# Group statistics, maxima and bias summed on VectorE by turning 32x32 squares, in a linear-attention block

## What is computed

```python
g = (x - mean_G(x)) / sqrt(var_G(x) + 1e-5)      # over the positions and the 8 channels of a group
q, k, v = split(g @ W_qkv)                        # 256 columns each
k = softmax(k, axis=n)                            # over the 4096 positions
context = einsum('nd,ne->de', k, v)
out = x + einsum('de,nd->ne', context, q) @ W_out + b_out
```

## Time and profile before

| | us |
|---|---|
| median of 3 runs | 1215.44 (1214.12 to 1215.74) |
| the profiled execution | 1214.93 |
| span in its trace, first to last instruction | 1213.2 |
| outside the span | 1.7 |

### The profile page before, as it was taken

The page is one execution under the profiler, slowest core; times in us unless marked ns, Lnnn a source line. Parts: engine busy times, 40 slices in busy tenths (PEclk is TensorE's granted clock), DMA queues, the critical chain, the costliest instruction groups (busy, mean ns, idle before and its releaser), DMA issues.

```text
span 1213.2 us, 21447 instructions
## 1 busy us (share of the span) xinstructions
PE 1190.1 (98%) x8460; PEld 1115.8 (92%) x8460; DVE 842.1 (69%) x1582; ACT 840.1 (69%) x1140; POOL 622.4 (51%) x288
## 2 busy tenths in 40 slices
PE   4999999999999999999999999999999999999998
PEld 4998999999899998999989999899999989999897
DVE  6877667676776767768776677766767676676551
ACT  5767768677685776757677686776857768577664
POOL 8664564635645355563655636356463564536520
PEclk9999999999999999999999999999999999999999
DMA  9448666576765758666486665867657576573524
GB/s 339 146 167 294 218 235 205 195 269 208 274 203 199 264 172 294 226 206 237 162 301 229 221 227 183 286 209 252 204 201 263 193 278 225 201 252 122 191 74 170
DMA packets 107077, 266.71 MB, mean 220 GB/s; under 512 B 10208, under 2 KB 10208, under 8 KB 106976
## 3 DMA queue, kind: packets, MB, share of 16 engines
q1 hardware_dynamic: 106976, 265.33, 63.5%
HBM read 198.18 MB, written 67.11 MB: 219 GB/s over the span
## 4 chain that ended last, share of the span: by engine, by line
PE 93%; DVE 2%; ACT 1%; POOL 1%; DMA 1%; issue 1%; SPq 0%; DVEq 0%; POOLq 0%; ACTq 0%
PE ps_k L399 29%; PE ps_e L564 19%; PE ps_e L573 10%; PE ps_g L492 5%; PE ps_e L480 5%; PE ps_e L492 5%; PE ps_e L482 5%; PE ps_g L480 4%; PE ps_g L482 4%; PE ps_g L511 1%; PE ps_g L528 1%; PE ps_g L542 1%; PE ps_g L534 1%; POOL x_lo L347 1%; DVE mx L892 1%
## 5 line engine op out<-in xcount | busy, mean ns | idle before, releaser
L341 POOL TENSOR_TENSOR xt_lo<-xt_raw,xt_hi 128x1024 fp32r<-128x1024 f32 x128 | 307.4, 2404 | 434.5 <-ACT xt_hi L676 309.1
L347 POOL TENSOR_TENSOR x_lo<-x_raw,x_hi 128x1024 fp32r<-128x1024 f32 x128 | 281.4, 2216 | 65.6 <-ACT x_hi L681 56.2
L892 DVE TENSOR_TENSOR mx<-ps_k,mx 128x256 f32<-128x256 f32 x480 | 203.3, 424 | 95.8 <-ACT e_raw L685 74.3
L733 ACT ACTIVATE o_stage<-ps_e,bias 128x512 f32<-128x512 f32 x253 | 170.9, 689 | 114.1 <-PE ps_e L573 114.1
L399 PE MATMUL ps_k<-wk_hi,xt_hi 128*128 128x256 f32 x1024 | 207.1, 284 | 1.0 <-DVE mx L892 0.7
L399 PE MATMUL ps_k<-wk_lo,xt_hi 128*128 128x256 f32 x1024 | 205.5, 283 | 0.0
L685 ACT ACTIVATE e_raw<-ps_k 128x512 f32<-128x512 f32 x256 | 141.4, 596 | 87.2 <-PE ps_k L399 87.2
L849 DVE BATCH_NORM_STATS2 bn<-xs 128x6 f32<-128x512 f32 x240 | 154.5, 686 | 40.7 <-DMA xs<-in_xt_dram 39.5
L693 ACT ACTIVATE e_hi<-e_raw 128x1024 fp32r<-128x1024 f32 x128 | 135.1, 1055 | 60.9 <-DVE e_raw L917 33.0
L399 PEld LDWEIGHTS ps_k<-wk_hi,xt_hi 128*128 128x128 f32 x1024 | 163.4, 190 | 8.7 <-issue 1.8
L399 PE MATMUL ps_k<-wk_hi,xt_lo 128*128 128x256 f32 x1024 | 158.2, 283 | 0.0
(11 more groups left out here) (129 smaller groups left out, 1992.7 us busy)
## 6 DMA issues: line engine op xcount, KB each, us to landing
xt_raw<-in_xt_dram SPq DMA_DIRECT2D x128, 512.0 KB, 4.3
x_raw<-in_xn_dram SPq DMA_DIRECT2D x128, 512.0 KB, 3.5
out_dram<-o_stage SPq DMA_DIRECT2D x127, 512.0 KB, 4.5
xs<-in_xt_dram SPq DMA_DIRECT2D x240, 256.0 KB, 5.1
w_setup<-in_w_dram SPq DMA_DIRECT2D x2, 256.0 KB, 10.1
out_dram<-o_stage SPq DMA_DIRECT2D x2, 256.0 KB, 2.0
wk<-in_w_dram SPq DMA_DIRECT2D x1, 256.0 KB, 9.9
wq_t<-in_w_dram SPq DMA_DIRECT2D x1, 256.0 KB, 10.9
```

What stands on the lines that cost most here:

```text
L341: nc.gpsimd.tensor_tensor(xt_lo[:, s], xt_raw[:, s], xt_hi[:, s].bitcast(F32), ALU.subtract).then_inc(xt_lo_ready, 1)
L347: nc.gpsimd.tensor_tensor(x_lo[:, s], x_raw[:, s], x_hi[:, s, :, 0:C].bitcast(F32), ALU.subtract).then_inc(x_lo_ready, 1)
L733: nc.scalar.activation(o_stage[:, u % O_SLOTS, h, :], src, ACT.Identity, bias=bias[:, h:h + 1]).then_inc(o_ready, 1)
L892: nc.vector.tensor_tensor(mx[:], tile, mx[:], ALU.max).then_inc(max_done, 1)
```

## The change

The averages over groups, the maxima and the bias no longer pass through TensorE, but for one matmul a block that spreads the maximum. In place of the 128x128 turn, VectorE turns 32x32 squares (`nc.vector.transpose`), so channel 32q+i comes to partition i of each quarter; it reduces along the row, moves the three upper quarters of the partitions down to the first (`move`, a reduction over one element), and reduces again. `block_diag` then writes the maxima (high and low part) on the diagonals of 64 x 256, and `spread_max` becomes one float32r matmul with ones. `group_sum` does the same for the group averages: turn, sum 8 neighbours, repeat each 8 times, turn back. `bias_of` is now a weighted sum over partitions of `ps_g0`, made by the same steps. Scales of the two blocks (`alpha`) are made on 32 partitions and spread by four moves. The last two statistics slices of the next image and `bn_sum` move from the end of the keys stage into the gather; `take_first` moves behind `e_low(b, 6)`. GpSimd waits for `diag_ready` ahead of two of its subtractions, and `rstd_of` moves two places back. ScalarE prepares two constants at the start. The same happens for image 0, whose order is written out apart.

```diff
-            def turn_max(b, blk):
-
-                to = max_psum(b, blk)
-                pe.wait_ge(max_done, b * (TILES * NCH) + TILES * HALF * (blk + 1))
-                for d in range(CB):
-                    last = nc.tensor.transpose(to[:, 0, d * P:(d + 1) * P], mx[:, d * P:(d + 1) * P], ident)
-                last.then_inc(t_ps, 1)
-
             def spread_max(b, blk):
 
-                to = max_psum(b, blk)
-                pe.wait_ge(m_blk_ready, b * 2 + (blk + 1))
-                for d in range(CB):
-                    last = nc.tensor.matmul(to[:, 1, d * P:(d + 1) * P],
-                                            m_blk[:, blk, d:d + 1].broadcast_to([P, P]), ident,
-                                            start=(d == 0), stop=True, skip_group_check=True)
-                last.then_inc(bc_ps, 1)
-
+                pe.wait_ge(diag_ready, b * 2 + (blk + 1))
+                nc.tensor.matmul(max_psum(b, blk)[:, 1, 0:C], one_r[0:2 * Q].broadcast_to([2 * Q, P]), diag,
+                                 start=True, stop=True).then_inc(bc_ps, 1)
...
-            def bias_sum(b, parity):
-                pe.wait_ge(m_full_ready, b + 1)
-                for h in range(CB):
-                    for c in range(CB):
-                        last = nc.tensor.matmul(ps_g0[:, 0, h:h + 1], m_full[:, c, h * P:(h + 1) * P],
-                                                neg_mean[:, parity, c:c + 1], start=(h == 0 and c == 0),
-                                                stop=(c == CB - 1), skip_group_check=True)
-                last.then_inc(bias_ps, 1)
...
                 n, np_ = b + 1, 1 - parity
+                pool.wait_ge(diag_ready, b * 2 + 2)
                 if more:
                     xt_low(n, np_, 0)
-                    if b:
-                        rstd_of(n, np_)
                 for j in range(HALF, NCH):
                     x_low(b, j)
-                    if b == 0 and j == NCH - 2:
+                    if more and j == (NCH - 2 if b == 0 else NCH - 3):
                         rstd_of(n, np_)
                 if more:
                     pool.wait_ge(wk_ready, n + 1)
@@ -388,6 +415,8 @@
                     for j in range(X_SLOTS):
                         x_low(n, j)
                     for j in range(3, NCH):
+                        if j == HALF + 1:
+                            pool.wait_ge(diag_ready, n * 2 + 1)
                         xt_low(n, np_, j)
 
...
+            def move(to, values):
+
+                return nc.vector.tensor_reduce(to, values.unsqueeze(len(values.shape)), AX_X, ALU.max)
...
+            def group_sum(n):
+
+
+                nc.vector.transpose(st_turned[:], st[:]).then_inc(st_turned_ready, 1)
+                dve.wait_ge(st_turned_ready, n)
+                nc.vector.tensor_reduce(st_sum[:], st_turned[:].rearrange("p (g i) -> p g i", i=GC), AX_X,
+                                        ALU.add).then_inc(st_sum_ready, 1)
+                dve.wait_ge(st_sum_ready, n)
+                move(st_held[:].rearrange("p (g i) -> p g i", i=GC),
+                     st_sum[:].unsqueeze(2).broadcast_to([P, Q // GC, GC])).then_inc(st_held_ready, 1)
+                dve.wait_ge(st_held_ready, n)
+                nc.vector.transpose(st_group[:], st_held[:]).then_inc(st_group_ready, 1)
+                dve.wait_ge(st_group_ready, n)
+
+            def stats_of(b, parity):
+                dve.wait_ge(mv_ready, b + 1)
+                group_sum(2 * b + 1)
+                mean_sum = st_group[:, 0:2 * CB].rearrange("p (c s) -> p c s", c=CB)[:, :, 0]
+                nc.vector.scalar_tensor_tensor(out=dev[:], in0=mean_sum, scalar=-1.0 / GC, in1=mv[:, :, 0],
+                                               op0=ALU.mult, op1=ALU.add)
+                nc.vector.tensor_scalar(neg_mean[:, parity, :], mean_sum, -1.0 / GC, None, ALU.mult).then_inc(mean_read, 1)
+                dve.wait_ge(var2_ready, b + 1)
+                group_sum(2 * b + 2)
+                nc.vector.tensor_scalar(var_eps[:], st_group[:, 2 * CB:3 * CB], 1.0 / GC, EPS, ALU.mult,
+                                        ALU.add).then_inc(var_eps_ready, 1)
...
             def block_max(b, blk):
-                src = max_psum(b, blk)
-                dve.wait_ge(t_ps, b * 2 + (blk + 1))
-                nc.vector.tensor_reduce(m_blk[:, blk, :], src[:, 0, 0:C].rearrange("p (d n) -> p d n", d=CB),
-                                        AX_X, ALU.max).then_inc(m_blk_ready, 1)
+
+
+                n = b * 2 + blk + 1
+                dve.wait_ge(max_done, n * (TILES * HALF))
+                nc.vector.transpose(turned[:], mx[:]).then_inc(turned_ready, 1)
+                dve.wait_ge(turned_ready, n)
+                nc.vector.tensor_reduce(quad[:, :, 0], turned[:].rearrange("p (q k) -> p q k", k=Q), AX_X,
+                                        ALU.max).then_inc(quad_ready, 1)
+                dve.wait_ge(quad_ready, n)
+                for r in range(1, QUADS):
+                    last = move(quad[0:Q, :, r], quad[r * Q:(r + 1) * Q, :, 0])
+                last.then_inc(quad_moved, 1)
+                dve.wait_ge(quad_moved, n)
+                nc.vector.tensor_reduce(m_blk[:, blk, :], quad[0:Q], AX_X, ALU.max).then_inc(m_blk_ready, 1)
+
+            def block_diag(b, blk):
+                n = b * 2 + blk + 1
+                dve.wait_ge(m_blk_ready, n)
+                move(m_parts[0:Q, :], m_blk[:, blk, :]).then_inc(m_part_hi_ready, 1)
+                dve.wait_ge(m_part_hi_ready, n)
+                nc.vector.tensor_tensor(m_parts[Q:2 * Q, :], m_blk[:, blk, :], m_parts[0:Q, :].bitcast(F32),
+                                        ALU.subtract).then_inc(m_part_lo_ready, 1)
+                if n == 1:
+                    dve.wait_ge(eye2_ready, 1)
+                dve.wait_ge(m_part_lo_ready, n)
+                nc.vector.tensor_tensor(diag.rearrange("p (q k) -> p q k", k=Q),
+                                        eye2[:].unsqueeze(1).broadcast_to([2 * Q, NQ, Q]),
+                                        m_parts[:].bitcast(F32).unsqueeze(2).broadcast_to([2 * Q, NQ, Q]),
+                                        ALU.mult).then_inc(diag_ready, 1)
...
+            def spread_scales(b):
+
+                dve.wait_ge(alpha_q_ready, b + 1)
+                by_quad = alpha_q[:].rearrange("p k (d r) -> p k d r", r=QUADS)
+                for r in range(QUADS):
+                    last = move(alpha[r * Q:(r + 1) * Q, :, :], by_quad[:, :, :, r])
+                last.then_inc(alpha_ready, 1)
...
+            def scale_mean(b, parity):
+                nc.vector.tensor_tensor(scaled_mean[:], neg_mean[:, parity, :], rstd[:, parity, :],
+                                        ALU.mult).then_inc(scaled_mean_ready, 1)
...
             def bias_of(b):
-                dve.wait_ge(bias_ps, b + 1)
-                dve.wait_ge(b_mean_ready, b + 1)
-                if not (isinstance(b, int) and b == 0):
+
+
+                dve.wait_ge(scaled_mean_ready, b + 1)
+                nc.vector.tensor_scalar(b_terms[:, 0, :], ps_g0[:, 0, 0:C], scaled_mean[:, 0:1], None,
+                                        ALU.mult).then_inc(b_first_ready, 1)
+                dve.wait_ge(b_first_ready, b + 1)
+                nc.vector.scalar_tensor_tensor(out=b_terms[:, 0, :], in0=ps_g0[:, 1, 0:C], scalar=scaled_mean[:, 1:2],
+                                               in1=b_terms[:, 0, :], op0=ALU.mult, op1=ALU.add).then_inc(b_terms_ready, 1)
+                dve.wait_ge(b_terms_ready, b + 1)
+                nc.vector.transpose(b_terms[:, 1, :], b_terms[:, 0, :]).then_inc(b_turned_ready, 1)
+                dve.wait_ge(b_turned_ready, b + 1)
+                nc.vector.tensor_reduce(b_quad[:, 0, :], b_terms[:, 1, :].rearrange("p (q k) -> p q k", k=Q), AX_X,
+                                        ALU.add).then_inc(b_quad_ready, 1)
+                dve.wait_ge(b_quad_ready, b + 1)
+                for r in range(1, QUADS):
+                    last = move(b_quad[0:Q, r, :], b_quad[r * Q:(r + 1) * Q, 0, :])
+                last.then_inc(b_moved, 1)
+                if b == 0:
+                    dve.wait_ge(b_loaded, 16)
+                else:
                     dve.wait_ge(o_ready, b * (CB * NCH))
-                nc.vector.tensor_tensor(bias[:], ps_g0[:, 0, 0:CB], b_mean[:], ALU.add).then_inc(bias_ready, 1)
+                dve.wait_ge(b_moved, b + 1)
+                nc.vector.tensor_reduce(b_all[:], b_quad[0:Q].rearrange("p r q -> p q r"), AX_X,
+                                        ALU.add).then_inc(b_all_ready, 1)
+                dve.wait_ge(b_all_ready, b + 1)
+                by_quad = b_all[:].rearrange("p (d r) -> p d r", r=QUADS)
+                for r in range(QUADS):
+                    last = move(bias[r * Q:(r + 1) * Q, :], by_quad[:, :, r])
+                last.then_inc(bias_ready, 1)
 
...
             def gather_steps(b, parity, more):
                 n, np_ = b + 1, 1 - parity
```

(38 more changed lines are left out.)

126 lines of the change are left out of this document (54 added, 72 removed).

## The result

The changed kernel takes **1261.7 us** (median of 4 runs, 1259.6 to 1264.0), the kernel before 1215.4 beside it: a ratio of 1.0384, 95% interval 1.0358 to 1.0411. (One further run of the kernel before took 4129 us and is left out of both figures.) The forecast was 1188, its range ended at 1211, and the sign was wrong. Most of the difference from the forecast is three effects: VectorE held up by GpSimd at two places, loads that come late behind a late bias, and a matmul that costs more than was taken for it. Both holds are decided by hundredths of a microsecond.

A forecast was written before the change was run, and what follows sets the result against it. TensorE, busy 98% of the span, was taken as the bound. From 1214.9 us, 37.7 saved on TensorE, plus 8.2 at the edges and 3 of small waits, gave 1188 us; range 1181 to 1211.

The forecast's parts named there:

- I take VectorE as winner of both: Gather: `dm` against `xt_low(n, 0)` and `dev` against `x_low(b, 5)`; VectorE wins the shared lock by hundredths of a microsecond.
- up to 0.17 of a GpSimd instruction passes before it needs the lock: Gather races: GpSimd's start leaves VectorE this grace, since `rstd` needed 0.54 of its 0.71 us after `e_low`'s end.
- mixed: Rival: images fall on either side of a race, or other waits sum to about 1 us each; 1195 to 1206, chance 0.13.
- Both races lost: Rival: `dm` and `dev` both wait for GpSimd in the gather; TensorE waits 2.6 us an image, 1224 us, chance 0.09.
- Covered by 1.0: Emit: VectorE's 2.9 us bias chain has the output buffer free at 383.1, before TensorE wants it at 384.1; last image excepted.
- small waits: TensorE waits where chains are thinly covered: 0.2 us an image, 3 us in all, range 0 to 5.
- The new spread at 0.12: Spreading the maxima: one 256-column matmul costs TensorE 0.12 us, as 24 such make a 2.87 us keys chunk.
- The maxima's 8.0 us of gain: Block 0's maxima leaving TensorE save 0.50 us net an image, 8.0 us in 16 images.
- the gather's 14.1: Maxima and statistics matmuls leaving the gather save TensorE 1.01 us net an image, 14.1 us in 14 images.
- the floor from distances: Distances between TensorE starts give 37.7 us saved: floor 1177 us, an image's stretch about 71.7 us.
- Image 0 loses 4 us: Image 0: GpSimd's `e_lo` subtractions beside low part and diagonal, three steps ahead of `shift(0, 6)`; bounds 0 and 8.
- The reason given for the late start: Start: `dev` waits for GpSimd's five subtractions until 17.2, so keys start 1.5 us later, plus 0.9 for slow matmuls.

The follow-up runs named there:

- e1: The changed kernel with `block_scales`, and so `dm`, ahead of `block_diag` in the gather: 1247.6 us, ratio 1.0270.
- e9: On top of e1, `st_group` and `dev` placed in a free part of PSUM instead of SBUF: 1221.7 us, ratio 1.0044.
- e9q: e9 with `xs` loads of images 2 to 15 cut to a quarter of their columns (wrong output): 1201.1 us, ratio 0.9876.
- e9q3: e9q with the diagonals on 128 partitions, so the spread matmul has 128 rows (wrong output): 1195.4 us, ratio 0.9831.
- e3: The changed kernel with the diagonals on 128 partitions, lower 64 zero, so the spread is a matmul of 128 rows: 1260.7 us, ratio 1.0376.
- e2: The changed kernel with the bias summed on TensorE again, as in the kernel before: 1255.3 us, ratio 1.0331.
- e11: e9 with the diagonals on 128 partitions, full computation: 1221.7 us, ratio 1.0049.

## Why the prediction was wrong

The account, from the change down to the forecast: the hold of `dm` 14.1 us (e1), the hold of `dev` 25.9 (e9), transfers behind the late bias 20.7 (e9q), rows of the spread 5.7 (e9q3), together 66.3 of the 73.7 us between 1261.7 and 1188. The terms depend on their order: e3 alone gave 1 us, e2 alone 6.4. The last two steps are measured on kernels that load less.

**The step that failed first is "I take VectorE as winner of both."** The times of the race were right: `dm` ready 0.11 us after the diagonal, GpSimd 0.08; the trace has GpSimd ahead by 0.03. What was wrong was the grace of "up to 0.17 of a GpSimd instruction passes before it needs the lock", taken from `rstd`, a power on two columns. For a subtraction the start counts: 0.03 us ahead was enough for `dm` in 15 of 16 images (the last has no `xt_low(n, 0)`), 0.08 ahead for `dev` in all 14 of e1. Nor did the race fall now one way, now the other: the distance was the same within 0.01 us in each image, so "mixed" deserved less and "both lost" far more than 0.09.

**Both races lost** was sized at 1224, 2.6 us an image. The two holds cost 40.0 us in fact, 2.5 to 2.7 an image in 15 or 16 images: the mechanism and its price were there, on the wrong side. The first half came as that rival has it: the shift at g + 7.3 (7.0 there), `e_low(b, 3)` behind `x_low(b, 4)` and done at g + 11.3 (11.0). The second didn't: with `dm` held, `dev` was held in only 3 images; only with `dm` free was it held in all of images 1 to 14 (e1).

**"Covered by 1.0"** for the bias failed in its scope. The chain took 3.4 us where 2.9 was costed, and the first output tile was there for TensorE all the same, but the step was wrong in that it asked only when TensorE wants the tile. Behind ScalarE's wait stand the first store and, behind that in the same queue, four loads; behind the bias on VectorE stand the next maxima and the statistics of `xs`. I named none of these. This is the 20.7 us, against 3 for all small waits.

**The new spread at 0.12** was taken from matmuls of 128 rows; with 64 it is 0.50. In 32 of them that is 12.2 us of TensorE's time. The maxima's 8.0 us of gain was thus about 2 (8.0 - 16 x 0.38), and the gather's 14.1 about 9 (14.1 - 14 x 0.38).

**What held.** Turns of 0.44 and 0.21 us, the diagonal after 2.47 (2.3), and the floor from distances: most images of e9q3 take 71.9 us or a little more, where 71.7 was forecast. The first gather of e9q3 begins at 48.13 instead of 46.72, 1.4 us later (by the sum 1.9: 2.4 at the start, less 0.5 for the maxima). The reason given for the late start was wrong: `dev` is hardly held there (0.34 us at 16.66 in the changed kernel); TensorE waits for the setup's weights and for ScalarE instead.

**Image 0, the last image and the clock.** "Image 0 loses 4 us" was an estimate between 0 and 8. Its first reason was right: in the changed kernel the low part of the maxima is held there by GpSimd's `e_lo` subtraction (1.38 us instead of 0.15). From its first gather matmul to the next image's, image 0 takes 76.5 us before, 85.7 in the changed kernel and 79.0 in e9q3; the sum has 78.2 (4 more, less 2.3 for its gather, its bias and the next maxima). In all kernels with the maxima on VectorE, TensorE waits in image 0 for the diagonal of block 1, and its granted clock falls during that wait or soon after. In e9q3, where `dm` stands ahead of the diagonal and is the one held:

```profile
55.02 1.39 DVE L945 TENSOR_TENSOR dm<-m_blk,m_all 32x16 f32<-32x16 f32 x1
...
57.18 0.58 PE L475 MATMUL ps_k<-u_hi,one_r 128*128 128x256 f32 x1 [3.77 <-DVE u_hi L935]
```

and the window of the lower clock, in the form of the earlier trace rows; behind the busy times stands the granted clock, 0.50, that is 1.2 GHz instead of 2.4:

```profile
55.70:62.50 6.80, 5.32 (x24) 5.32 (x25) 6.69 (x14) 5.50 (x7) 5.97 (x3) 0.50 0.24 77
```

In it the gather's matmuls come 0.21 us apart instead of 0.12. e9q3 has this clock for 6.8 us here and for 3.4 in the last image, after a wait of 2.2 us for `o_stage`. The changed kernel has it for 3.4 us from 56.9, after a wait of 3.5 us; for 6.8 from 73.9, around a wait of 4.6 us for `e_lo`; and for 3.4 in the last image. The kernel before has the full clock up to 1210 us. The prediction had no term for this. By these rows it costs at most half of the stretch, an estimate: up to 5.1 us in e9q3 and up to 6.8 in the changed kernel. No run separates it from the waits.

The last 7.4 us between e9q3 and the forecast I didn't take apart further. What the trace shows of them are the waits for `x_lo` (4.1 us) and the last image: from its first gather matmul to the end it takes 62.0 us where the sum has 58.9, with 1.2 us of waiting for its diagonal, 2.2 for `o_stage` and 3.4 us of the lower clock.

## What to carry to other kernels

Before moving small steps to VectorE beside a busy GpSimd, list those with two inputs in SBUF and every tensor_scalar from SBUF to SBUF, and price each at a whole GpSimd instruction unless an order of semaphores, not hundredths of a microsecond, keeps them apart; a free corner of PSUM for their operands removed the second hold here. A chain is covered only if everything queued behind each engine that waits for it is covered too: the store and the loads behind it count. When a mended part moves the time by nothing (e3, e11), look for the time in the next wait, and try the part again after that one is gone (e9q3). And a wait of some microseconds on TensorE can cost more than its length, since the granted clock can fall to the lower level with it, as in image 0 here.
